# A two-layer Mamba/attention/mixture-of-experts kernel on one core: a scan group's output product summed in PSUM and copied by ScalarE, attention masks on GpSimd, packed attention averages

## The chip, the core and the metric

The kernel runs on one core of one Trainium2 chip. The metric is the device time of one execution in microseconds; three runs of the kernel before are known. The core has five queues of instructions: TensorE (PE, matmuls and their weight loads), VectorE (DVE), ScalarE (ACT), GpSimd (POOL) and SyncE (SP, which starts DMAs). Each runs its own instructions in the order in which they were written; between queues there are semaphores only. GpSimd works on SBUF tiles alone in this kernel.

## The reference, cut to what matters

Input x is 8 sequences of 256 tokens of 128 channels. Layer 0 normalises, runs a forward and a backward Mamba block and a top-2 mixture of experts and adds all up. Layer 1 runs a switch router with capacity 32 and its experts, and two attention blocks in a row. The parts that the change touches:

```python
# layer 0, for the forward and the backward direction
h = jnp.exp(dt_t[..., None] * A) * h + (dt_t * u_t)[..., None] * B_t[:, None, :]   # 16 states, 256 channels
y_t = jnp.einsum('bdn,bn->bd', h, C_t)
y = (y + u * Dp) * silu(z)
return jnp.einsum('bld,ed->ble', y, Wout)        # the output product; both directions are added to the rest
# layer 1, twice: global (causal) and then local (causal, window 32)
scores = jnp.einsum('bhqd,bhkd->bhqk', q, k) / np.sqrt(HD)     # 16 heads of 8, 4 key/value heads
scores = jnp.where(mask, scores, jnp.float32(-1e+30))
probs = softmax(scores);  out = jnp.einsum('bhqk,bhkd->bhqd', probs, v) @ wo
mask = (diff >= 0) & (diff < WIN)                # local; global is diff >= 0
```

## The kernel before, in words

**Scan stage.** Tokens are in four pairs of sequences (512 columns). A *scan group* g is one pair and one direction: groups 0 to 3 forward, 4 to 7 backward. Each group has 16 states N, and each state two halves of 128 channels. Per state and half, ACT computes the decays (line 878, in `decay`), POOL multiplies `dtu` by a broadcast row of B (line 682), DVE runs the scan (line 1203), and the result is multiplied by the row of C, half 0 by DVE (line 1211), half 1 by POOL (line 690). Of three states in four PE makes the drive of half 0 instead of POOL, as a matmul or a transpose (`turn_drive`, lines 1796 and 1798). PE sums the products over states in PSUM banks 4 and 5 (`add_y`, line 1818; line 1812 begins a group with the D term).

The rest of a group's work is spread over the states of the group before or after: depthwise convolution and projection u (lines 1728, 1776, 1779), z (1744), x (1748), dt (1752), all through one PSUM bank, `side`, that its users take in a fixed order (`SIDE`). Three states into a group DVE gates the previous group's sum (`gate_y`, line 1243), PE transposes it (line 1835), ACT copies it to `yT`, and PE's `finish` (line 1844) multiplies it by `Wout` into `side`, two matmuls for each of four token tiles. DVE then adds `side` to the running total `acc` (line 1255). ACT's Silu of u and z (lines 830, 832), between two table loads, stands in the same stretch, and so does dt: PE line 1752, ACT lines 851, 853, 855, DVE line 1185, after which POOL makes the next group's `dtu` (line 759).

`timeline()` writes out the order of this work once for PE and once for the readers of PSUM. `tensor_order` sets, for each state N, whether PE adds state N-3 or makes the drive of N+1 first: the drive is first where N modulo 16 is in `TURN_FIRST`.

**Attention stage.** 16 rounds b (8 global, then 8 local), one per sequence, each of three 128x128 blocks of keys and queries (`BLOCKS`: two on the diagonal, one under it, in that order), each block in two *units* of two key/value heads: 96 units. A unit is: PE writes a mask of 0 and -30000 into PSUM (lines 2077 and 2082; not for the full block under the diagonal) and adds the scores on top (lines 2088 and 2091), ACT takes the exponential into `probs` (line 1110, 1,024 elements per partition; 256 elements of 32 partitions for a local block under the diagonal, the *corner*). PE then averages the values, four matmuls of 512 columns per block (`average`, lines 2111 and 2114), into one bank for each 128 queries. Each such bank is copied by ACT (line 1117), transposed back by PE in four parts (line 2121) and divided by its row sums by DVE (lines 1634 and 1637). A matmul writes 32 rows per key/value head of which 9 hold values and the row sum. PE's, ACT's and DVE's preparation for later sequences (rms, T, L, Q, K, sqr, inv, split, turn) and the output projection (O1, O2) stand at places that `attention_timeline` gives. GpSimd only raises to the power -0.5 there (line 695).

## Time and profile before

| | us |
|---|---|
| median of 3 runs | 784.01 (783.31 to 787.82) |
| the profiled execution | 782.85, of which its span is 781.1 |
| the last scan of layer 0 ends | at 512.3 |
| router and experts of layer 1 | to 583.7 |
| attention: first to last exponential | 583.70 to 770.9 |
| after the last exponential | to 781.1 |

Over the span PE is busy 84%, DVE 75%, ACT 69% and POOL 53%; GpSimd does nearly nothing after 515 us. Times in rows are microseconds from the start of the span. In the rows below "x8" is eight merged instructions; a 128x128 float32 matmul that isn't a transpose shows as two of them. Durations of neighbours overlap a little, so what one instruction takes of its queue is read from two starts. The number in square brackets at a row's end is the time for which the engine had been idle, with what released it.

### The profile page before, as it was taken

To read this page: it belongs to the slowest core of one execution; us is meant where nothing else is said; L and a number is where in the kernel's file an instruction comes from. 1 tells how busy PE (TensorE), PEld (TensorE's weight loads), DVE (VectorE), ACT (ScalarE), POOL (GpSimd) and SP (SyncE) were. 2 spreads that over 40 slices of the span, in tenths; PEclk is the share of its full clock that TensorE was granted. 3 is DMA by queue.
4 is the path that set the end of the run, shared out by engine and by line. 5 is a ranking of instruction groups with operands and counts; after the bars stand their busy time and mean duration, and the time that the engine had idled before them with its cause. 6 is when DMAs were issued, how large, how long until landed. Compare 5 with 4: busy or idle time off the path is not lost.

```text
span 781.1 us, 13600 instructions
## 1 busy us (share of the span) xinstructions
PE 657.2 (84%) x4531; PEld 478.5 (61%) x4531; DVE 585.5 (75%) x863; ACT 540.6 (69%) x1021; POOL 416.9 (53%) x362
## 2 busy tenths in 40 slices
PE   4899977889898797888888967789888788888986
PEld 2588946658676585676776757677673334344433
DVE  7435679998999999999999998983335545655542
ACT  3465475877969878688798897825637757766663
POOL 6400168898998999989999899930000000000000
PEclk8799999899999999999999998999999999989998
DMA  6323577577596886857868668720200000000000
GB/s 199 109 82 115 153 165 214 164 206 222 151 248 184 195 255 152 231 181 178 258 168 221 205 156 235 198 108 28 82 1 0 2 1 2 1 1 2 15 14 28
DMA packets 81412, 100.15 MB, mean 128 GB/s; under 512 B 32560, under 2 KB 37816, under 8 KB 81344
## 3 DMA queue, kind: packets, MB, share of 16 engines
q1 hardware_dynamic: 81344, 99.29, 45.2%
q8 instruction: 37, 0.61, 0.3%
q14 instruction: 31, 0.25, 0.1%
HBM read 96.12 MB, written 3.24 MB: 127 GB/s over the span
## 4 chain that ended last, share of the span: by engine, by line
PE 43%; DVE 18%; issue 18%; ACT 13%; POOL 7%; DMA 0%; DVEq 0%; POOLq 0%; ACTq 0%
DVE ps L1203 5%; PE ps L1818 5%; PE ps L1869 3%; DVE hc L1211 3%; DVE moe L1203 3%; POOL drive L682 3%; PE ps L1884 3%; POOL hc L690 3%; PE ps L1796 3%; PE ps L2114 3%; PE ps L1748 2%; PE ps L1844 2%; PE ps L2091 2%; PE ps L1728 2%; PE ps L2021 2%
## 5 line engine op out<-in xcount | busy, mean ns | idle before, releaser
L682 POOL TENSOR_TENSOR drive<-dtu,b_sb 128x512 f32<-128x512 f32 x160 | 203.1, 1278 | 0.5 <-PE ps L1818 0.4
L690 POOL TENSOR_TENSOR hc<-moe,c_sb 128x512 f32<-128x512 f32 x128 | 163.3, 1276 | 19.2 <-DVE moe L1203 18.9
L1203 DVE TENSOR_TENSOR_SCAN moe<-ps,drive 128x512 f32<-128x512 f32 x128 | 153.4, 1199 | 0.0
L1818 PE MATMUL ps<-ident,hc 128*128 128x128 f32 x1024 | 139.3, 284 | 0.6 <-POOL hc L690 0.6
L1818 PEld LDWEIGHTS ps<-ident,hc 128*128 128x128 f32 x1024 | 122.5, 147 | 25.8 <-issue 19.9
L1110 ACT ACTIVATE probs<-ps 128x1024 f32<-128x1024 f32 (+1 forms) x96 | 87.6, 915 | 62.6 <-PE ps L2091 50.8
L878 ACT ACTIVATE ps<-dt,negA 128x510 f32<-128x510 f32 x160 | 106.5, 677 | 29.2 <-DVE moe L1203 28.5
L1203 DVE TENSOR_TENSOR_SCAN ps<-decay_sb,ps 128x512 f32<-128x512 f32 x96 | 117.2, 1221 | 12.4 <-PE ps L1796 11.6
L695 POOL TENSOR_TENSOR stat<-stat,halfc 128x4 f32<-128x4 f32 x7 | 7.1, 1008 | 190.9 <-DVE stat L1472 190.9
L1211 DVE TENSOR_TENSOR hc<-ps,c_sb 128x512 f32<-128x512 f32 x128 | 85.3, 666 | 0.0
L878 ACT ACTIVATE decay_sb<-dt,negA 128x510 f32<-128x510 f32 x96 | 68.3, 711 | 16.3 <-DVE ps L1203 16.3
L1796 PE MATMUL ps<-xm,dtuT 128*128 128x128 f32 x384 | 56.2, 293 | 12.2 <-DVE hc L1211 12.0
L909 ACT ACTIVATE scaled<-dtuT,bT 128x128 f32<-128x128 f32 x192 | 60.1, 389 | 0.6 <-PE ps L1798 0.6
L1796 PEld LDWEIGHTS ps<-xm,dtuT 128*128 128x128 f32 x384 | 51.0, 207 | 14.7 <-issue 14.7
L2114 PE MATMUL ps<-probs,v_ring 128*32 128x512 f32 x320 | 44.4, 626 | 8.6 <-DVE moe L1637 8.6
L1798 PE MATMUL ps<-ident,scaled 128*128 128x128 f32 x192 | 30.1, 280 | 25.5 <-DVE hc L1211 25.0
L1605 DVE CAST qT<-ps 128x512 f16<-128x512 f32 x32 | 22.1, 689 | 29.8 <-PE ps L2012 29.7
L1798 PEld LDWEIGHTS ps<-ident,scaled 128*128 128x128 f32 x192 | 22.1, 145 | 32.4 <-issue 24.9
L1203 DVE TENSOR_TENSOR_SCAN ps<-ps,drive 128x512 f32<-128x512 f32 x32 | 39.1, 1222 | 2.0 <-ACT ps L878 2.0
L813 ACT ACTIVATE hT<-ps,wbuf 128x256 f32<-128x256 f32 x64 | 25.8, 476 | 16.2 <-PE ps L1869 16.2
L768 POOL TENSOR_TENSOR seqstat<-seqstat,halfc 128x2 f32<-128x2 f32 x8 | 5.6, 698 | 58.3 <-DVE seqstat L1401 58.3
L1884 PEld LDWEIGHTS ps<-wbuf,hT 128*128 128x128 f32 x256 | 30.8, 192 | 3.1 <-issue 2.5
(281 smaller groups left out, 1224.3 us busy)
## 6 DMA issues: line engine op xcount, KB each, us to landing
b_sb<-bc_rows SPq DMA_DIRECT2D x128, 256.0 KB, 4.0
c_sb<-bc_rows SPq DMA_DIRECT2D x128, 256.0 KB, 4.0
xm<-spot_rows SPq DMA_DIRECT2D x48, 256.0 KB, 4.3
wbuf<-in_pack SPq DMA_DIRECT2D x16, 514.0 KB, 3.4
wbuf<-in_pack SPq DMA_DIRECT2D x8, 512.0 KB, 5.0
spot_rows<-c_sb SPq DMA_DIRECT2D x6, 256.0 KB, 4.5
x_sb<-in_x SPq DMA_DIRECT2D x4, 256.0 KB, 3.7
out<-x_sb SPq DMA_DIRECT2D x4, 256.0 KB, 2.3
```

The lines of the kernel that those rows point to most:

```text
L682: pool.tensor_tensor(drive_of(N, half), dtu[:, N // STATES % 2, half], b_sb[:, N % B_RING], ALU.mult) \
L690: pool.tensor_tensor(hc[:, 2 * (N % DEEP) + half], h_of(q), c_sb[:, N % C_RING], ALU.mult).then_inc(sem["hc_pooled"], 1)
L878: act.activation(seqs(decay_bank(q))[:, :, lo:lo + SEQ - 1], seqs(dt[:, g % 2, half])[:, :, lo:lo + SEQ - 1], ACT.Exp, scale=negA[:, g // ...
L909: last = act.activation(scaled[:, n % 2, block], dtuT[:, block], ACT.Copy, scale=bT[:, t, j:j + 1])
L1110: act.activation(probs[keys, t % 3, heads_u, 0:width], ps[keys, heads_u, 0:width], ACT.Exp, scale=HD ** -0.5).then_inc(sem["probs_ready"], 1)
L1203: dve.tensor_tensor_scan(h_of(q)[:, turn], decay_bank(q)[:, turn], source[:, turn], 0.0, ALU.mult, ALU.add).then_inc(sem["scan_done"], 1)
L1211: dve.tensor_tensor(hc[:, 2 * (N % DEEP)], h_of(q), c_sb[:, N % C_RING], ALU.mult).then_inc(sem["hc_ready"], 1)
L1796: last = pe.matmul(ps[:, H_BANKS[N % OWN_H], block], dtuT[:, block], spots[:, n % SPOT_RING, block], start=True, stop=True)
L1798: last = pe.transpose(ps[:, H_BANKS[N % OWN_H], block], scaled[:, n % 2, block], ident[:])
L1818: last = pe.matmul(ps[:, Y_BANK + half, block], hc[:, 2 * (N % DEEP) + half, block], ident[:], start=False, stop=True, is_transpose=True, ...
L1884: last = pe.matmul(bank[:, t * D:(t + 1) * D], hT[:, k, c, t * P:(t + 1) * P], wbuf[:, r, HIDDEN + CHUNKS + c * D:HIDDEN + CHUNKS + (c + 1 ...
L2114: last = pe.matmul(ps[g, AV_BANK + qt], v, probs[:, t % 3, kv], start=(t % 3 < 2), stop=(t % 3 != 1))
```

## The change

- `finish` on PE, for groups 0 to 6, adds `acc` into the same PSUM bank with four more matmuls by the identity, and ACT copies the bank to `acc` or `x_sb`. For groups 0 to 5 the copy stands in `side_part` between the Silu of u and that of z; for 6 it has a place of its own. DVE keeps the addition of group 7 alone.
- `TURN_FIRST` gains states 5 and 9, and DVE's `gate_y` stands before the scan of half 0, no longer between the halves.
- No mask goes through PE. After the exponential GpSimd sets what is hidden to zero in `probs`, in place, with `affine_select` (the function `hide`): one pass for each diagonal unit of the global rounds, two with a wait between them for the local ones, one small pass for a local corner unit. `average` waits for it, and stands one unit later in PE's order. Three loads of masks go.
- Averages are packed: heads go in two groups of 256 columns, the second with its values 16 rows higher (`VPAD`), so that one bank holds both 128-query halves of a sequence. There are eight matmuls of 256 columns per block for four of 512, and one ACT copy, one set of four transposes and one reciprocal per round for two.
- In attention `rms`, `T`, the copies and the order of k and q in `split` move; T, L and O1 are read before the exponential of their slot.

```diff
-TURN_FIRST = (4, 6, 8)
+TURN_FIRST = (4, 5, 6, 8, 9)
...
-        for n, at in ((2 * b, 4), (2 * b + 1, 8)):
-            put(6 * b + at + 2, "back", n)
-            put(6 * b + at, "copy", n)
+        put(6 * b + 11, "back", b)
+        put(6 * b + 9, "copy", b)
...
-        if at % 2 and 1 < at <= UNITS1 + 1:
-            unit.append(("average", at // 2 - 1))
-        first = [ev for ev in here if ev[0] == "turn"]
+        if at % 2 == 0 and 2 < at <= UNITS1 + 2:
+            unit.append(("average", at // 2 - 2))
+        first = [ev for ev in here if ev[0] in ("turn", "T", "L", "O1")]
...
+            def hide(U):
+                t = U // 2
+                l, own = t >= 3 * SEQS, BLOCKS[t % 3] != (0, 1)
+                if not l and not own:
+                    return
+                pool.wait_ge(sem["probs_ready"], U + 1)
+                after(pool, "probs_seen", seen_before(U))
+                heads_u = slice(2 * (U % 2), 2 * (U % 2) + 2)
+                keys, n = (slice(0, P), P) if own else (slice(P - WINDOW, P), WINDOW)
+                p = probs[keys, t % 3, heads_u, 0:GROUP * n].rearrange("p g (j q) -> p g j q", j=GROUP)
+                rows = [[0, 2], [0, GROUP]]
+                if own:
+                    first = pool.affine_select(p, p, rows + [[1, n]], ALU.is_ge, 0.0, base=0, channel_multiplier=-1)
+                    if not l:
+                        first.then_inc(sem["probs_seen"], 1)
+                        return
+                    first.then_inc(sem["probs_cut"], 1)
+                    pool.wait_ge(sem["probs_cut"], cut_before(U) + 1)
+                pool.affine_select(p, p, rows + [[-1, n]], ALU.is_ge, 0.0, base=WINDOW - 1 if own else -1, channel_multiplier=1) \
+                    .then_inc(sem["probs_seen"], 1)
...
                     act.activation(u_s[:, g % 2], u_s[:, g % 2], ACT.Silu).then_inc(sem["u_ready"], 1)
+                    if g > 1:
+                        finish(g - 2)
                     act.wait_ge(sem["side_free"], SIDE["z", g, 1] + 1)
...
+            def finish(g):
+                act.wait_ge(sem["side_ready"], SIDE["finish", g] + 1)
+                act.activation((x_sb if g >= PAIRS else acc)[:, 4 * (g % PAIRS):4 * (g % PAIRS) + 4],
+                               side.rearrange("p (t d) -> p t d", d=D), ACT.Copy).then_inc(sem["side_free"], 1)
...
+                if N > STATES and N % STATES == LAG:
+                    gate_y(N // STATES - 1)
                 scan(N, 0)
                 turn_boundary(2 * N)
-                if N > STATES and N % STATES == LAG:
-                    gate_y(N // STATES - 1)
                 scan(N, 1)
...
                     for half in range(HALVES):
                         last = pe.matmul(side[:, t * D:(t + 1) * D], yT[:, half, t * P:(t + 1) * P],
-                                         w_out[:, g // PAIRS, half], start=(half == 0), stop=(half == HALVES - 1))
+                                         w_out[:, g // PAIRS, half], start=(half == 0), stop=(half == HALVES - 1 and g == STEPS - 1))
+                    if g < STEPS - 1:
+                        if g < PAIRS:
+                            pe.wait_ge(sem["ln0_added"], SEQS)
+                        else:
+                            pe.wait_ge(sem["side_free"], SIDE["finish", g - PAIRS] + 1)
+                        last = pe.matmul(side[:, t * D:(t + 1) * D], ident[:], acc[:, 4 * (g % PAIRS) + t], start=False, stop=True)
...
-                        for rows in HALF_ROWS:
-                            keys = rows if kv == kvs[0] else HALF_ROWS[rows is HALF_ROWS[0]]
-                            pe.matmul(ps[keys, kv], ident16[rows, rows],
-                                      masks[rows, l if kv == kvs[0] else 3 + l].unsqueeze(1).broadcast_to([P // 2, GROUP, P]),
-                                      start=True, stop=False)
...
                 pe.wait_ge(sem["probs_ready"], 2 * t + 2)
+                pe.wait_ge(sem["probs_seen"], seen_before(2 * t + 2))
...
-                if t % 3 < 2:
-                    after(pe, "heads_done", 2 * (b - 1) + qt + 1)
+                if t % 3 == 0:
+                    after(pe, "heads_done", 2 * (b - 1))
```

The first place is PE in scan group 3, from the second transpose of the gated sum (line 1835) to the projection x. Before (L1844 is `finish`, L1748 x, L1752 dt, L1796 a drive):

```order
L1835 MATMUL ps<-ident,yg 128x128 x4
L1818 MATMUL ps<-ident,hc 128x128 x8
L1744 MATMUL ps<-w_in,xmT 128x128 x4
L1818 MATMUL ps<-ident,hc 128x128 x8
L1796 MATMUL ps<-xm,dtuT 128x128 x4
L1744 MATMUL ps<-w_in,xmT 128x128 x4
L1796 MATMUL ps<-xm,dtuT 128x128 x4
L1818 MATMUL ps<-ident,hc 128x128 x8
L1844 MATMUL ps<-w_out,moe 128x128 x8
L1818 MATMUL ps<-ident,hc 128x128 x8
L1796 MATMUL ps<-xm,dtuT 128x128 x4
L1748 MATMUL ps<-u_s,w_x 104x512 x2
```

The same stretch of PE in the changed kernel, where line 1884 is `finish`, 1891 its new matmuls, 1836 a drive and 1858 a sum:

```order
L1784 MATMUL ps<-w_in,xmT 128x128 x4
L1836 MATMUL ps<-xm,dtuT 128x128 x4
L1858 MATMUL ps<-ident,hc 128x128 x8
L1784 MATMUL ps<-w_in,xmT 128x128 x4
L1836 MATMUL ps<-xm,dtuT 128x128 x4
L1858 MATMUL ps<-ident,hc 128x128 x8
L1884 MATMUL ps<-w_out,moe 128x128 x2
L1891 MATMUL ps<-acc,ident 128x128
```

The drive of state 6 now stands before a sum, not behind it, and `finish` is four times (two matmuls and one more). Between `finish` and dt the order holds the same work as before, with the drive of state 10 one sum earlier.

The second place is PE in the attention stage, about one global round. Before, a diagonal unit is line 2082 (masks) and 2091, and each round has two sets of line 2121:

```order
L2114 MATMUL ps<-probs,v_ring 32x512 x4
L2121 MATMUL ps<-ident,avT 128x128 x4
L2012 MATMUL ps<-ident,qs 128x128 x4
L2091 MATMUL ps<-qT,kT 128x512 x4
L2114 MATMUL ps<-probs,v_ring 32x512 x4
L2121 MATMUL ps<-ident,avT 128x128 x4
L2012 MATMUL ps<-ident,qs 128x128 x4
L2082 MATMUL ps<-masks,ident 64x512 x4
L2091 MATMUL ps<-qT,kT 128x512 x2
```

In the changed kernel (2127 scores, 2155 averages, 2163 transposes back, 2058 and 2052 turns):

```order
L2155 MATMUL ps<-probs,v_all 32x256 x8
L2052 MATMUL ps<-ident,ks 128x128 x2
L1998 MATMUL ps<-w_kvu,latT 128x64 x4
L2127 MATMUL ps<-qT,kT 128x512 x2
L2058 MATMUL ps<-ident,qs 128x128 x4
L2127 MATMUL ps<-qT,kT 128x512 x2
L2155 MATMUL ps<-probs,v_all 32x256 x8
L2163 MATMUL ps<-ident,avT 128x128 x4
L2127 MATMUL ps<-qT,kT 128x512 x2
```

There are no rows for masks, eight short matmuls stand for four long ones, and one set of transposes back belongs to a round.

The third place is GpSimd in the local rounds, where before it had nothing but line 695. One round is now (line 798 the first pass, 804 the second and that of the corner):

```order
L798 AFFINE_SELECT probs<-probs 128x1024
L804 AFFINE_SELECT probs<-probs 128x1024
L798 AFFINE_SELECT probs<-probs 128x1024
L804 AFFINE_SELECT probs<-probs 128x1024
L798 AFFINE_SELECT probs<-probs 128x1024
L804 AFFINE_SELECT probs<-probs 128x1024
L798 AFFINE_SELECT probs<-probs 128x1024
L804 AFFINE_SELECT probs<-probs 128x1024
L804 AFFINE_SELECT probs<-probs 32x2x128 x2
```

Eight passes over 1,024 elements and two over 256 are what a local round adds to that queue.

## Rows read from the trace of the kernel before

**Rows 1.** Windows: us; busy PE, PEld, DVE, ACT, POOL; clock, DMA. Scan, global, local.
```profile
275.50:324.50 49.00, 41.49 (x274) 32.23 (x272) 47.76 (x57) 39.06 (x75) 46.88 (x39) 0.97 0.76 203
583.70:679.87 96.17, 79.08 (x646) 35.31 (x646) 53.39 (x111) 68.31 (x94) 4.03 (x4) 0.98 0.00 1
679.87:770.90 91.03, 80.62 (x699) 40.06 (x699) 46.70 (x101) 60.86 (x91) 2.02 (x2) 0.94 0.04 10
```

**Rows 2.** Timeline, DVE in scan group 3: start, duration, instruction, idle time before it.
```profile
272.72 1.27 DVE L1243 TENSOR_TENSOR yg<-ps,z_s 128x512 f32<-128x512 f32 x2
...
282.07 1.23 DVE L1203 TENSOR_TENSOR_SCAN ps<-decay_sb,ps 128x512 f32<-128x512 f32 x1 [0.72 <-PE ps L1796]
...
287.78 0.69 DVE L1255 TENSOR_TENSOR acc<-acc,ps 128x512 f32<-128x512 f32 x1
288.39 1.23 DVE L1203 TENSOR_TENSOR_SCAN ps<-ps,drive 128x512 f32<-128x512 f32 x1
```

**Rows 3.** The chain of waits through the same group, start, us, what.
```profile
283.21 1.21 DVE moe L1203
...
285.70 2.05 PE ps L1844 x16
287.75 0.87 PE ps L1818 x8
288.62 0.89 PE ps L1796 x8
289.51 1.72 PE ps L1748 x4
...
296.80 0.72 ACT decay_sb L878
...
297.54 0.07 DVE ps L1203
```

**Rows 4.** Timeline, DVE's longest waits for PE in groups 1, 4 and 7.
```profile
179.69 1.23 DVE L1203 TENSOR_TENSOR_SCAN ps<-decay_sb,ps 128x512 f32<-128x512 f32 x1 [1.09 <-PE ps L1796]
183.80 1.23 DVE L1203 TENSOR_TENSOR_SCAN ps<-decay_sb,ps 128x512 f32<-128x512 f32 x1 [1.19 <-PE ps L1796]
333.02 1.23 DVE L1203 TENSOR_TENSOR_SCAN ps<-decay_sb,ps 128x512 f32<-128x512 f32 x1 [1.02 <-PE ps L1796]
480.88 1.23 DVE L1203 TENSOR_TENSOR_SCAN ps<-decay_sb,ps 128x512 f32<-128x512 f32 x1 [1.41 <-PE ps L1796]
```

**Rows 5.** Timeline, PE at the gate of groups 3 and 4.
```profile
273.54 0.63 PE L1835 MATMUL ps<-ident,yg 128*128 128x128 f32 x4 [1.82 <-DVE yg L1243]
...
324.61 0.66 PE L1835 MATMUL ps<-ident,yg 128*128 128x128 f32 x4 [0.78 <-ACT u_s L822]
```

**Rows 6.** Lines by form, global rounds, then local: count, busy, mean ns, idle before.
```profile
L2114 PE MATMUL ps<-probs,v_ring 128*32 128x512 f32 x176 | 24.3, 624 | 4.4 <-DVE moe L1637 4.4
...
L2114 PE MATMUL ps<-probs,v_ring 128*32 128x512 f32 x144 | 20.1, 629 | 4.2 <-DVE moe L1637 4.2
...
L2077 PE MATMUL ps<-masks,ident 128*32 128x128 f16 x32 | 4.6, 224 | 0.0
```

**Rows 7.** Timeline, PE in the global rounds.
```profile
641.04 0.41 PE L2082 MATMUL ps<-masks,ident 64*64 64x512 f16 x4
641.38 0.39 PE L2091 MATMUL ps<-qT,kT 32*128 32x512 f16 x2
...
642.70 0.66 PE L2121 MATMUL ps<-ident,avT 128*128 128x128 f32 x4
643.19 0.39 PE L2012 MATMUL ps<-ident,qs 128*128 128x128 f16 x4
```

**Rows 8.** Timeline, GpSimd: one fill of 512 and of 1,024 elements.
```profile
0.74 0.53 POOL L642 MEMSET c_sb<- 128x512 f32 x1 [0.29 <-POOLq L2214]
...
525.75 0.95 POOL L775 MEMSET v_ring<- 128x1024 f32 x1
```

**Rows 9.** The page's costliest groups: GpSimd's product of two tiles.
```profile
L690 POOL TENSOR_TENSOR hc<-moe,c_sb 128x512 f32<-128x512 f32 x128 | 163.3, 1276 | 19.2 <-DVE moe L1203 18.9
```

More of the change, by code:

```diff
@@ L267, in attention_timeline @@
         unit = [("unit", at)] if 0 <= at < UNITS1 else []
-        if at % 2 and 1 < at <= UNITS1 + 1:
-            unit.append(("average", at // 2 - 1))
-        first = [ev for ev in here if ev[0] == "turn"]
+        if at % 2 == 0 and 2 < at <= UNITS1 + 2:
+            unit.append(("average", at // 2 - 2))
+        first = [ev for ev in here if ev[0] in ("turn", "T", "L", "O1")]
         order += here + unit
-        readers += first + unit + [ev for ev in here if ev[0] != "turn"]
+        readers += first + unit + [ev for ev in here if ev not in first]
     return order, readers
@@ L291, with seen_before, cut_before @@
 PREP = {ev: n for n, ev in enumerate(ev for ev in FILL + AT_ORDER if ev[0] in ("T", "L", "Q", "K", "O1", "O2"))}
+def seen_before(U):
+    return sum(V // 2 >= 3 * SEQS or V // 2 % 3 < 2 for V in range(U))
+def cut_before(U):
+    return sum(V // 2 >= 3 * SEQS and V // 2 % 3 < 2 for V in range(U))
 def shared_before(q):
@@ L780, in _ @@
                     rms_pow(ev[1])
+                    pool.wait_ge(sem["rms_pow"], ev[1])
+                elif ev[0] == "unit":
+                    hide(ev[1])
         @block.scalar
@@ L983, in _ @@
                     copy_y(ev)
+                elif ev == ("finish", STEPS - 2):
+                    finish(STEPS - 2)
                 elif ev[0] == "xt":
@@ L2001, in turn @@
                 first = 2 * (b % 2)
-                pe.wait_ge(sem["qk_split"], 2 * G + 2)
+                pe.wait_ge(sem["qk_split"], 2 * G + (2 if part else 1))
                 after(pe, "turn_copied", TURN["turn", b, part])
@@ L2115, in average, with turn_back @@
                 last.then_inc(sem["av_done"], 1)
[L2117 to L2121 removed]
+            def turn_back(b):
+                pe.wait_ge(sem["av_copied"], b + 1)
+                for n in range(4):
+                    last = pe.transpose(ps[:, AV_BANK + b % 2, n * P:(n + 1) * P], avT[:, b % 2, n * P:(n + 1) * P], ident[:])
```

116 lines of the change are left out of this document (54 added, 62 removed).

## The prediction

> **What bounds the kernel now.** I read the windows by stage first. In a scan group of 49.0 us DVE is busy 47.8 and POOL 46.9 [rows 1]: DVE sets the pace there, and every microsecond in which it waits is lost. In the attention rounds no engine is full, but PE comes nearest: 79.1 of 96.2 us in the global rounds and 80.6 of 91.0 in the local ones, with ACT at 68.3 and 60.9 and POOL at 4.0 and 2.0 [rows 1]. There TensorE and ScalarE hand units to each other, and GpSimd is free.
>
> The timeline of DVE in the scan shows one recurring gap, the wait for the drive of state 6, 0.72 us in group 3 [rows 2], and more in groups 1, 4 and 7: 1.09 and 1.19, 1.02, 1.41 [rows 4]. Group 6 repeats group 1 within 0.01, groups 2 and 5 repeat group 3, group 7 has 0.16 more. That makes 9.3 us in all.
>
> The chain of waits shows what else is tight. From the scan at 283.21 it runs over ACT's decay and copy of z, then on PE without a hole over `finish` (285.70), a sum, a drive, x (289.51), two sums, a drive and dt, ends on ACT with the decay at 296.80 (0.72 us), and lets DVE's scan go at 297.54, 0.02 us behind it [rows 3]. DVE itself had no gap between its own scans there. So two strings of equal length run side by side in that stretch of every group but the last: DVE's own work, with the addition of `finish` in it, and the PE-ACT string, with the matmuls of `finish` in it.
>
> **The scan stage, part by part.**
>
> *The addition leaves DVE.* It takes 0.61 us of its queue, from 287.78 to 288.39 [rows 2]. But it stood on one of two equal strings, and the other grows: `finish` gets four more float32 matmuls of 128x128. Four such matmuls are one drive, 0.89 us [rows 3]. PE goes from `finish` to dt without idling, so dt comes 0.9 later and DVE waits, first at a decay that ACT now makes late, then at dt. ACT's copy of the bank, 0.5 us and a wait of about 0.8 for PE before it, falls in the time for which the x projection is awaited anyway, so it adds nothing to the string. Groups 1 to 6: +0.9 x 6 = +5.4 us. Group 7 has no dt, there DVE gains its 0.6. If the string had slack that I don't see, the six groups would give 0.6 each back instead: bounds -3.6 and +5.4, and I take +5.4, as the slack shown is 0.02. Net +4.8.
>
> *The gate moves ahead of the scan of half 0.* The two gate operations begin at 272.72 and the scan before them is one pitch earlier, 1.1 us. PE had been idle for 1.82 us when they came [rows 5], so all that follows on PE, up to the drive of state 6, comes 1.1 earlier. In group 4 the transposes were released by ACT's copy of u, not by the gate [rows 5], so nothing moves there.
>
> *The drive of state 6 goes before a sum.* A sum of eight transposes is 0.87 [rows 3], which is what the drive gains. Together 2.0 us, or 0.9 in group 4. Groups 2, 3, 5 and 7 then lose their whole gap (0.7 x 3 + 1.6), groups 1 and 6 2.0 of 2.3 each, group 4 0.9 of 1.0: -8.6 us. POOL has 2.1 us to spare in a group and doesn't stop this. Bounds: 0 (another wait lies right behind) to -9.3. I take -8.6, since the idle before the gate is longer than the shift.
>
> Scan stage: +4.8 - 8.6 = **-3.8 us**.
>
> **The attention stage.**
>
> *Masks off PE.* Four mask matmuls take 0.34 us of the queue, from 641.04 to 641.38 [rows 7]. 32 diagonal units in each half of the stage: -10.9 in the global rounds, as much in the local ones. The 16 corner units had 32 small ones, busy 4.6 us with overlaps [rows 6]; I take 3.5.
>
> *Packing.* A set of transposes back takes 0.49 (642.70 to 643.19) [rows 7], eight fewer in each half, -3.9. The waits of the average for DVE's division of the bank, 4.4 in the global rounds and 4.2 in the local ones [rows 6], go, since the next round has a bank of its own. Against it stand four more matmuls in each of 48 averages with the same columns. I put 0.1 each, between 0 and the 0.5 of a whole set of four transposes: +2.4 a half. ACT also gets rid of 16 copies, DVE of 16 small operations; they bound nothing.
>
> *Global rounds.* 10.9 + 3.9 + 4.4 - 2.4 = 16.8 us come off PE. ACT with 68.3 busy in 96.2 becomes the neighbour, so not all is won: the same sum times PE's busy share, 0.82, is 13.8, and the earlier T and L would add a little. **-15**, bounds -10 and -22.
>
> *GpSimd's passes.* No row shows `affine_select`. The nearest below is a fill, one stream, 0.95 us for 1,024 elements [rows 8]; from 512 to 1,024 it grows by 0.42, so 0.11 is fixed. The nearest above is a product of two tiles, 1.28 for 512 [rows 9], thus 2.5 for 1,024. A pass has one tile to read and one to write, and a comparison of the position; it is nearer to the fill, and I take c = 1.1. For what lies between two passes, each with a wait, I add 0.1, as much as the fixed part of a fill. In the global rounds 32 passes are 38 us of 81 and hide behind units.
>
> *Local rounds.* PE without masks needs 91.0 - 10.9 - 3.5 - 3.9 - 4.2 + 2 = about 71 us. GpSimd needs 64 x 1.2 + 16 corner passes at a quarter of the elements, 16 x 0.46, + 2 for its powers [rows 1] = 86.2. **GpSimd is the new bound**, and the local rounds take 86.2, not 91.0: **-4.8**; bounds -14 (c = 0.95) and +90 (c = 2.5). What waits behind a late pass is the average on PE's queue, and with it the scores behind it.
>
> *Tail.* After the last unit there is a pass, a longer average and both halves of the output in one copy: **+1**, bounds 0 and 3.
>
> *Loads.* Three loads of masks fewer at the end of the scan, hidden beside it: 0. The router and experts get the L projection of the second preparation instead of the attention stage: 0.
>
> **Sum.** 782.85 - 3.8 - 15 - 4.8 + 1 = 760.3 for an execution like the profiled one, which is 1.2 below the median shown: **761.5 us**.
>
> **The rivals.**
>
> *GpSimd is slow and the kernel is slower.* Each microsecond more on c makes the local rounds longer by 64 + 4 = 68 us. The total is back at 784 when c is 1.43. With c in the middle of the two rows, 1.73, it is 761 + 43 = 804; with 2.5 it would be 857. For it: two passes per local unit on one queue, and the only arithmetic on full tiles that GpSimd shows runs at more than twice the time per element of the fill. Against: those have two inputs, this has one. By over 1% it is slower from c = 1.55 on; chance **0.20**.
>
> By the Trainium skill (GPSIMD Engine Reference, 3.1) the tight loop of a one-input operation is bound by its ports at 1.03 cycles of 1.2 GHz per element for up to two operations, and takes at best about 1.8 for three or more. No row here shows which holds for a mask that depends on position. By the first c would be an estimated 0.99 and the sum about 754, by the second an estimated 1.65 and the sum about 799.
>
> *About the same.* c between 1.31 and 1.55, or c of 1.1 with half of the rest lost, because DVE stands at `rms` until GpSimd's power comes, which now queues behind passes, and the turned copies that PE needs stand behind it. 776 to 792. Six such waits of some 2 us are possible; DVE is idle 43 us of the global rounds [rows 1], which speaks against it. Chance **0.13**.
>
> *The scan gives nothing.* The gaps of groups 1, 6 and 7, longer than the others [rows 4], show PE slower behind the gate there; if it gets slower still, only half of the 8.6 comes back: +4.8 - 4.3, total 766. This lies inside the forecast's range.
>
> *More than forecast.* c at the fill's 0.95 makes GpSimd's local sum 76, the dt string turns out to have slack, and the global rounds give 20: 761 - 10 - 8 - 5 = 738. Chance of less than 740: **0.05**.
>
> *The move does not do what it says.* The addition is meant to leave the bound engine, but its matmuls land on an equal string. That is in the forecast already.
>
> **How the numbers follow.** Forecast case, 740 to 776, 0.62; more than forecast 0.05; about the same 0.13; slower 0.20. The likeliest case gives 761.5. The range leaves out 0.05 below 740 and some 0.13 above 800: 740 to 800. A change of 1%, 8 us, is what these runs can tell. Faster by over 1% (below 776) 0.67, within 1% 0.13, slower 0.20.
>
> **What the changed profile would show.** A pass of 1,024 elements near 1.1 us, GpSimd busy over 9 tenths of the local rounds and PE idle there at the averages, released by GpSimd; DVE in the scan without gaps before state 6, but with new waits of half a microsecond or more for ACT's decays and at dt, some 0.9 us later after the copy of z than before; groups 2, 3 and 5 as long as before within 0.3 us, groups 1 and 6 shorter by over 1. The prediction is wrong if a pass is far from 1.1 us, if PE's saving in the global rounds comes back as ACT's, or if dt doesn't move.

## The result, and the profile after

The change made the kernel slower by 0.6%: 788.39 us (785.0 to 790.44, 20 runs) against 783.17 for the kernel before, a ratio of 1.0063 with a 95% interval of 1.0045 to 1.008. The forecast was 761.5. The profiled execution took 786.54 us, its span is 784.7 (781.1 before).

To compare stages over all kernels, I cut the span at two events that every one of them has: the first exp of attention and the first corner exp (32x256, four units into the local rounds); the last cut is the end of the last exp. These are the windows of the kernel before (from the first exp to the first corner exp, which I call the global stretch; to the end of the last exp, the local stretch; to the end, the tail; columns as in [rows 1]):

```profile
583.70:690.37 106.67, 89.09 (x734) 40.36 (x734) 58.29 (x122) 75.89 (x103) 4.03 (x4) 0.98 0.00 1
690.37:770.90 80.53, 70.62 (x613) 35.01 (x611) 41.80 (x90) 53.27 (x82) 2.02 (x2) 0.94 0.04 11
770.90:781.10 10.20, 3.83 (x30) 2.65 (x28) 2.48 (x6) 1.19 (x2) 0.00 (x0) 0.74 0.09 26
```

And of the changed kernel:

```profile
577.33:674.20 96.87, 78.25 (x750) 40.89 (x754) 59.87 (x114) 70.55 (x94) 47.01 (x41) 0.91 0.00 1
674.20:770.05 95.85, 66.54 (x618) 36.98 (x607) 46.26 (x83) 49.29 (x74) 79.18 (x76) 0.74 0.03 9
770.05:784.70 14.65, 6.79 (x48) 4.30 (x48) 2.50 (x7) 1.19 (x2) 1.94 (x3) 0.50 0.06 18
```

All up to the first exp is 6.4 us shorter, the global stretch 9.8 shorter, the local one 15.3 longer and the tail 4.5 longer: +3.6. In the local stretch GpSimd (fifth busy column) goes from 2 to 79 us, TensorE does 4 us less, and its granted clock falls from 0.94 to 0.74.

**The scan** went as the working had it. DVE's waits from 150 to 500 us in the kernel before, by what it waited for (total us, times, longest); the first line sums [rows 4] and their like:

```profile
DVE ps L1203 <- PE ps L1796: 9.3, 10, 1.4
DVE ps L1203 <- ACT decay_sb L878: 0.7, 2, 0.6
```

and after, where the drive of state 6 has lost its wait and the new ones are at ScalarE's decays and at dt:

```profile
DVE ps L1245 <- ACT decay_sb L918: 3.8, 8, 0.5
DVE moe L1245 <- ACT ps L918: 2.9, 6, 0.5
DVE dt L1227 <- ACT dt_a L889: 2.0, 6, 0.3
DVE ps L1245 <- ACT ps L918: 1.5, 1, 1.5
DVE ps L1245 <- PE ps L1836: 0.3, 1, 0.3
```

This window leaves out group 0. There the kernel before has 2.3 us more than every other profile of this document, and it isn't the code: run 10, which has the scan as before, takes 52.34 us for the group where the kernel before takes 54.70, and TensorE's clock differs. The same ten microseconds in the kernel before, then in run 10:

```profile
120.00:130.00 10.00, 7.87 (x52) 7.24 (x51) 9.90 (x14) 4.34 (x7) 7.91 (x8) 0.83 0.63 193
```

```profile
120.00:130.00 10.00, 7.87 (x64) 6.89 (x63) 9.90 (x14) 4.25 (x7) 7.90 (x8) 1.00 0.71 207
```

So of the 6.4 us ahead of the first exp 2.3 seem to belong to the profiled execution of the kernel before and not to the change.

**A pass** takes 1.09 us alone and 1.17 on average, where the forecast took 1.1. GpSimd's groups in the attention stage (count, busy, mean ns, idle before):

```profile
L798 POOL TENSOR_SCALAR_AFFINE_SELECT probs<-probs 128x1024 f32<-128x1024 f32 x64 | 74.6, 1165 | 82.2 <-ACT probs L1152 56.9 <-issue 20.1
L804 POOL TENSOR_SCALAR_AFFINE_SELECT probs<-probs 128x1024 f32<-128x1024 f32 x32 | 37.6, 1175 | 2.2
L804 POOL TENSOR_SCALAR_AFFINE_SELECT probs<-probs 32x256 f32<-32x256 f32 x16 | 10.0, 625 | 6.2 <-ACT probs L1152 4.2 <-POOL probs L804 0.4
```

**What holds the local rounds** shows at the `rms` of the last but one preparation. GpSimd, then DVE, then TensorE in the same 15 us (start, duration, instruction, idle before it):

```profile
688.45 1.09 POOL L798 TENSOR_SCALAR_AFFINE_SELECT probs<-probs 128x1024 f32<-128x1024 f32 x1
689.62 1.09 POOL L804 TENSOR_SCALAR_AFFINE_SELECT probs<-probs 128x1024 f32<-128x1024 f32 x1
690.68 1.01 POOL L702 TENSOR_TENSOR stat<-stat,halfc 128x4 f32<-128x4 f32 x1
691.76 0.96 POOL L804 TENSOR_SCALAR_AFFINE_SELECT probs<-probs 32x256 f32<-32x256 f32 x1
694.83 0.45 POOL L804 TENSOR_SCALAR_AFFINE_SELECT probs<-probs 32x256 f32<-32x256 f32 x1 [2.12 <-ACT probs L1152]
```

```profile
688.50 1.07 DVE L1511 TENSOR_SCALAR stat<-stat 128x4 f32<-128x4 f32 x1
691.72 0.69 DVE L1517 TENSOR_TENSOR xm<-acc,stat 128x512 f32<-128x512 f32 x1 [2.15 <-POOL stat L702]
```

```profile
687.46 0.66 PE L2163 MATMUL ps<-ident,avT 128*128 128x128 f32 x4
692.55 1.09 PE L1994 MATMUL ps<-ident,xm 128*128 128x128 f32 x4 [4.44 <-DVE xm L1517]
...
694.87 1.94 PE L2155 MATMUL ps<-probs,v_all 128*32 128x256 f32 x16
696.73 2.08 PE L2000 MATMUL ps<-w_q,xmT 128*128 128x128 f32 x8
```

DVE's variance (line 1511) is ready at 689.57, but GpSimd still has passes and reaches the power (line 702) at 690.68; `xm` follows at 691.72, T on TensorE at 692.55. T stands ahead of scores in TensorE's queue, so no unit is made meanwhile, and then GpSimd, the engine that was late, has nothing to do: 2.12 us at 694.83, and again at 696.07 and 700.48. TensorE comes out of the hole at its lower level: T takes 1.09 where it takes 0.63 elsewhere in the same kernel, an average 1.94 where it takes 1.07.

Two more readings bear on this. DVE waits for the power 1.12 us in each of the four preparations of the global rounds, and 2.15 and 5.75 us in the two of the local ones. And of the 10.2 us for which GpSimd waits in the local stretch 9.6 lie in the 9 us behind these two `xm`; from 730 us on, when nothing is prepared any more, it waits 0.6 us in all. What TensorE waits for most in the local stretch are the passes, at the averages, as the prediction said:

```profile
PE ps L2155 <- POOL probs L804: 14.7, 7, 3.2
PE ps L1994 <- DVE xm L1517: 8.0, 2, 4.4
```

### The profile page after: what moved, and what is told of

Read it like the earlier page. It is cut to its first block and busy times, and to the rows that moved or that the text cites. A ratio compares the mean times of both kernels' runs of the same rounds, so it can differ in the third digit from the quotient of the medians.

```text
span 784.7 us, 13926 instructions
## 1 busy us (share of the span) xinstructions
PE 646.9 (82%) x4619; PEld 482.7 (62%) x4619; DVE 586.2 (75%) x840; ACT 534.4 (68%) x1012; POOL 537.3 (68%) x474
## 5 line engine op out<-in xcount | busy, mean ns | idle before, releaser
L798 POOL TENSOR_SCALAR_AFFINE_SELECT probs<-probs 128x1024 f32<-128x1024 f32 x64 | 74.6, 1165 | 82.2 <-ACT probs L1152 56.9
L918 ACT ACTIVATE ps<-dt,negA 128x510 f32<-128x510 f32 x160 | 106.4, 677 | 26.3 <-DVE moe L1245 25.5
L1152 ACT ACTIVATE probs<-ps 128x1024 f32<-128x1024 f32 (+1 forms) x96 | 85.3, 915 | 43.5 <-PE ps L2127 32.7
L1253 DVE TENSOR_TENSOR hc<-ps,c_sb 128x512 f32<-128x512 f32 x128 | 84.9, 663 | 0.0
L918 ACT ACTIVATE decay_sb<-dt,negA 128x510 f32<-128x510 f32 x96 | 68.3, 711 | 15.3 <-DVE ps L1245 15.3
L2155 PE MATMUL ps<-probs,v_all 128*32 128x256 f32 x640 | 52.5, 454 | 21.2 <-POOL probs L804 16.4
L1836 PE MATMUL ps<-xm,dtuT 128*128 128x128 f32 x384 | 52.9, 282 | 11.1 <-DVE hc L1253 11.1
L1836 PEld LDWEIGHTS ps<-xm,dtuT 128*128 128x128 f32 x384 | 47.4, 194 | 14.6 <-issue 14.6
L804 POOL TENSOR_SCALAR_AFFINE_SELECT probs<-probs 128x1024 f32<-128x1024 f32 (+1 forms) x48 | 47.6, 992 | 8.4 <-ACT probs L1152 4.2
L2155 PEld LDWEIGHTS ps<-probs,v_all 128*32 128x32 f32 x640 | 19.7, 122 | 40.2 <-issue 26.1
```

The source lines that it names most:

```text
L798: first = pool.affine_select(p, p, rows + [[1, n]], ALU.is_ge, 0.0, base=0, channel_multiplier=-1)
L804: pool.affine_select(p, p, rows + [[-1, n]], ALU.is_ge, 0.0, base=WINDOW - 1 if own else -1, channel_multiplier=1) \
L918: act.activation(seqs(decay_bank(q))[:, :, lo:lo + SEQ - 1], seqs(dt[:, g % 2, half])[:, :, lo:lo + SEQ - 1], ACT.Exp, scale=negA[:, g // ...
L1152: act.activation(probs[keys, t % 3, heads_u, 0:width], ps[keys, heads_u, 0:width], ACT.Exp, scale=HD ** -0.5).then_inc(sem["probs_ready"], 1)
L1253: dve.tensor_tensor(hc[:, 2 * (N % DEEP)], h_of(q), c_sb[:, N % C_RING], ALU.mult).then_inc(sem["hc_ready"], 1)
L1836: last = pe.matmul(ps[:, H_BANKS[N % OWN_H], block], dtuT[:, block], spots[:, n % SPOT_RING, block], start=True, stop=True)
```

## Experiments

Each run stands beside runs of the kernel before on the same chip, and the ratio is to those. Runs 1, 3 and 5 form a ladder from the kernel before to the changed one. A step between two runs of the ladder is good to some 3 or 4 us by their intervals. Windows are of one profile each: the global stretch of the changed kernel is 96.87 us, and those of runs 9, 5 and 7, which differ from it only in how the last four units of the stretch are masked, are 99.76, 99.98 and 102.28. So differences of up to 5 us between single global stretches prove nothing.

**1. The scan part alone** (the attention stage of before):

```
-TURN_FIRST = (4, 6, 8)
+TURN_FIRST = (4, 5, 6, 8, 9)
...
+   last = pe.matmul(side[:, t * D:(t + 1) * D], ident[:], acc[:, 4 * (g % PAIRS) + t], start=False, stop=True)
```

> The kernel before with the scan part of the change alone (the sum of finish on TensorE with ScalarE's copy, the gate ahead of the scan of half 0, the drive of state 6 ahead of the sum); its attention stage is that of before. In the changed kernel's profile the first exp of attention begins 6.4 us earlier. If the scan part is what it looks like there, this is 777 us, 5 to 7 below the kernel before. Rival: the attention stage of the kernel before starts from another phase and takes some back, or the scan's gain there came with the other edits (the fill of the router and experts): 780 or more.

780.43 us, ratio 0.9953 (0.9928 to 0.9977), so -3.7 us; the forecast's term was -3.8. I had expected 777. The profiled run has the first exp at 577.96, 5.7 us earlier than before (2.3 of it in group 0), the same global stretch (106.70), and a local stretch and a tail that are 1.3 and 0.8 longer (81.85 and 10.99).

**2. The two moves of order alone**, `finish` added by DVE as before:

```
-TURN_FIRST = (4, 6, 8)
+TURN_FIRST = (4, 5, 6, 8, 9)
...
+if N > STATES and N % STATES == LAG:
+    gate_y(N // STATES - 1)
 scan(N, 0)
 turn_boundary(2 * N)
-if N > STATES and N % STATES == LAG:
-    gate_y(N // STATES - 1)
 scan(N, 1)
```

> The kernel before with the two moves of order alone (the gate ahead of the scan of half 0, the drive of state 6 ahead of the sum), while DVE keeps the addition of finish. If the sum of finish on TensorE lengthens a string as long as DVE's own, as the prediction had it (+4.8), this is some 5 us below the run with the whole scan part: 771 to 773. Rival: DVE is the bound alone and the finish move is worth 0.6 a group: then it is 3 to 4 us above the run with the whole scan part, 780 to 781.

772.46 us, ratio 0.986 (0.9821 to 0.9898): -11.0. DVE's waits in the scan:

```profile
DVE ps L1203 <- PE ps L1796: 1.4, 2, 1.1
DVE ps L1203 <- ACT decay_sb L878: 0.7, 2, 0.5
```

2.1 us instead of 10.5 in the changed kernel. So the addition that leaves DVE costs 7.3 us (0.9953 - 0.986), because its matmuls lie on the string to dt. The theory that DVE alone is the bound falls. The length of each scan group, from its first scan to the next group's (us, one profile each):

| group | 0 | 1 | 2 | 3 | 4 | 5 | 6 | 7 |
|---|---|---|---|---|---|---|---|---|
| kernel before | 54.70 | 50.79 | 49.13 | 50.43 | 49.66 | 49.14 | 51.07 | 48.89 |
| run 10, scan as before | 52.34 | 50.79 | 49.13 | 50.41 | 49.66 | 49.13 | 51.06 | 48.81 |
| run 2 | 52.41 | 48.32 | 48.32 | 49.60 | 48.79 | 48.32 | 48.60 | 48.29 |
| run 1 | 52.36 | 49.21 | 49.21 | 50.48 | 49.31 | 49.21 | 49.51 | 48.98 |
| changed kernel | 52.41 | 49.21 | 49.22 | 50.48 | 49.78 | 49.22 | 49.50 | 48.31 |

In group 7 of run 1 DVE waits once for a late decay, which it doesn't in run 2:

```profile
DVE ps L1213 <- ACT ps L886: 1.6, 1, 1.6
```

**3. The masks back on TensorE**, all else of the change kept:

```
-   elif ev[0] == "unit":
-       hide(ev[1])
+   pe.matmul(ps[keys, kv], ident16[rows, rows], masks[rows, ...], start=True, stop=False)
```

> The changed kernel with the masks back on TensorE as in the kernel before, and all else of the change kept (scan part, packed averages, moved order of the attention stage). Theory 1 (GpSimd's passes lose the time): 783 - 6 for the scan - some 6 to 12 for the packing: 765 to 771, and the granted clock of the local rounds is back at 0.9. Theory 2 (moved order and packing lose it): 778 or more, with TensorE's waits of 2.6 us at T before DVE's xm still there in the global rounds.

772.31 us, ratio 0.9858 (0.9826 to 0.989), a little above the range of theory 1. Theory 2 falls: packing and the moved slots don't lose the time. Its windows, cut as above (this profiled execution, 768.83 us, was the shortest of its six):

```profile
577.14:684.12 106.98, 92.72 (x896) 45.01 (x896) 57.34 (x114) 71.17 (x93) 4.03 (x4) 0.92 0.01 1
684.12:756.95 72.83, 66.94 (x764) 35.45 (x764) 40.03 (x84) 49.11 (x74) 2.02 (x2) 0.95 0.04 12
```

Against the kernel before the local stretch is 7.7 shorter and the global one not at all.

**4. No passes at all**, no wait for them: the masking is left out.

```
-   hide(ev[1])
...
-   pe.wait_ge(sem["probs_seen"], seen_before(2 * t + 2))
```

> The changed kernel without any of GpSimd's mask passes and without the wait for them: it leaves the masking out. Theory 1 (the passes on GpSimd hold up the units, by their own sum in the local rounds and by standing ahead of GpSimd's power for rms): local rounds fall from 104.7 to about 72, global ones from 88.7 to about 82, the tail by 2: 745 to 752. Theory 2 (the moved order and the packed averages lose the time: rms and T two slots later, one copy for both halves): the global rounds stay at 88 and the local ones at 85 or more: 768 or above.

759.33 us, ratio 0.9673 (0.9636 to 0.9709). The passes of the change cost 0.039, 30 us. The local stretch is 71.97, the tail 10.12. Theory 1 had the total too low by 7, theory 2 too high by 9. The global stretch is 101.62 and so no shorter than with passes: TensorE still waits 2.7 to 2.8 us at T four times there. (This profiled execution, 763.75 us, was the longest of its six.)

**5. Passes in the global rounds, TensorE's masks in the local ones:**

```
-   if not l and not own:
+   if l or not own:
        return
```

> The changed kernel with GpSimd's passes in the global rounds alone and the masks on TensorE in the local ones. Theory 1 (the loss of the change sits in the local rounds, where GpSimd has two passes a unit): the stretch from the first corner exp to the last exp falls from 95.9 to the 72.8 of the run with all masks on TensorE, the tail from 14.7 to 10.1: 788.4 - 23 - 4.6 = 761; the global rounds keep the 96.9 from the first exp to the first corner exp. Rival (the clock: less work on TensorE leaves it at its low level, and what the masks cost comes back): 768 to 772, as with all masks on TensorE.

763.02 us, ratio 0.9727 (0.9693 to 0.976). In the global rounds the passes give 0.0131, 10 us, against TensorE's masks (run 3 less this run); in the local rounds they cost 0.0336, 26 us (1.0063 - 0.9727). The whole loss is there:

```profile
577.96:677.94 99.98, 82.08 (x772) 42.01 (x772) 60.28 (x114) 70.30 (x94) 42.13 (x36) 0.90 0.00 1
677.94:751.88 73.94, 67.93 (x764) 35.96 (x764) 40.03 (x84) 49.07 (x74) 2.01 (x2) 0.93 0.04 12
```

**6. rms and T earlier**, in the changed kernel:

```
-for name, at in (("rms", -15), ("T", -13), ...
+for name, at in (("rms", -17), ("T", -14), ...
```

> The changed kernel with the slots of rms and T back at -17 and -14, where the kernel before has them; all else of the change kept. TensorE waited at T for DVE's xm 2.6 to 2.8 us four times in the global rounds and 3.5 to 4.4 in the local ones. Theory 1 (the shorter way from rms to T makes the holes, and in the local rounds the passes that stand ahead of GpSimd's power make them longer): the global rounds fall by 5 to 11, the local ones by some 8: 770 to 776. Rival (in the local rounds GpSimd's passes are the bound by their sum alone): only the global part comes back, and the local rounds stay at 100 or more: 778 to 783.

785.81 us, ratio 1.0033 (1.0013 to 1.0053). Only 0.003, some 2 us, comes back: both readings had more, 770 to 776 and 778 to 783. The local stretch is 92.58 us. **The same with TensorE's masks:**

> The kernel with the masks back on TensorE and all else of the change, and with rms and T at -17 and -14. In the run without this edit TensorE waited 11.0 us at T for DVE's xm in the global rounds and 2.7 in the local ones. Theory 1: the holes go, and the granted clock in the rounds that had them rises: 8 to 12 us below that run's 772.3, 760 to 764. Rival (the holes took the place of waits of the same size elsewhere, 15 us of them in the kernel before for the division, the latent copy and the keys): within 2 us of 772.

769.93 us, ratio 0.9818 (0.9786 to 0.985), an interval that overlaps that of run 3. I had expected 760 to 764, or 770 to 774 if the slots do nothing. The slots are not the cause of the loss.

**7. One pass instead of two** on each whole local unit; the window's mask on the diagonal units is left out.

```
-   if not l:
-       first.then_inc(sem["probs_seen"], 1)
-       return
-   first.then_inc(sem["probs_cut"], 1)
-   pool.wait_ge(sem["probs_cut"], cut_before(U) + 1)
+   first.then_inc(sem["probs_seen"], 1)
+   return
```

> The changed kernel with one of GpSimd's two passes on each whole local unit; it leaves out the window's mask on the diagonal units. GpSimd's own sum in the local rounds falls from 84 to 84 - 32 x 1.2 = 46 us. Theory A (the sum of the passes is the bound there, with the holes at rms as their consequence, since a unit waits two passes): local from the first corner exp 73 to 76, total 762 to 766. Theory B (a pass of any number behind the exp makes the way from a unit to its average, and so rms to T, longer): local 82 or more, total 772 or above.

762.98 us, ratio 0.9764 (0.9744 to 0.9783); the local stretch is 68.47. Theory B falls: a pass behind the exp isn't the trouble, the second one is. The tail is 12.03.

**8. The power of rms on ScalarE** for groups 4 to 7, both passes kept:

```
+   elif kind == "pow":
+       act.wait_ge(sem["rms_var"], G)
+       act.activation(stat[:, 0, rows], stat[:, 2, rows], ACT.Ln).then_inc(sem["rms_ln"], 1)
+       act.wait_ge(sem["rms_ln"], G - 3)
+       act.activation(stat[:, 3, rows], stat[:, 0, rows], ACT.Exp, scale=-0.5).then_inc(sem["rms_pow"], 1)
```

> The changed kernel with the power of rms of groups 4 to 7 on ScalarE (Ln and Exp, as it does for q and k) in a slot of its own, so that it no longer stands behind GpSimd's passes. If the in-order queue of GpSimd makes the holes (TensorE waits at T 4.4 and 3.5 us for xm, ScalarE 8.7 at its longest for T, GpSimd idle for 10 us in the local rounds in all), GpSimd then runs through: local falls by 8 to 10, total 778 to 780. Rival (the holes come from the units' rate, as ScalarE's square and DVE's sums also queue behind late units): within 3 us of 788.

774.48 us, ratio 0.9923 (0.9896 to 0.995): 0.014, 11 us, where 8 to 10 were expected, by taking four instructions of 1.0 us off a queue and `xm` off the slot of the sums. GpSimd has the same passes. The two stretches:

```profile
578.07:670.81 92.74, 75.86 (x742) 39.02 (x746) 59.80 (x113) 71.22 (x98) 44.59 (x39) 0.93 0.01 1
670.81:758.35 87.54, 64.09 (x622) 36.30 (x621) 46.88 (x85) 50.42 (x78) 77.44 (x74) 0.80 0.04 10
```

From the end of ScalarE's square to its copy of T are 3.4 us here (684.92 to 688.30), 6.0 in the change (687.68 to 693.68):

```profile
684.29 0.63 ACT L1068 ACTIVATE sq<-acc 128x512 f32<-128x512 f32 x1
685.95 0.21 ACT L1071 ACTIVATE stat<-stat 128x4 f32<-128x4 f32 x1 [1.03 <-DVE stat L1518]
...
688.30 0.69 ACT L1076 ACTIVATE xmT<-ps,cols 128x512 f32<-128x512 f32 x1 [1.50 <-PE ps L2004]
```

The local stretch falls by 8.3; the 4.1 of the global one are within its scatter. What remains above the 72.8 with TensorE's masks is GpSimd's own sum: 77.4 busy, 3.1 in waits for exps, and the other 7 in gaps of some 0.1 between instructions. The waits were 10.2 in the change.

**9. Masks in both places** in the local rounds, to see what the low clock does:

```
+elif kt == qt and l:
+    for rows in HALF_ROWS:
...
+        pe.matmul(ps[keys, kv], ident16[rows, rows], masks[rows, ...], start=True, stop=False)
```

> The changed kernel with the masks of the local rounds on TensorE too, beside GpSimd's passes, so that TensorE has some 14 us of matmuls more there and GpSimd the same passes. The granted clock of the local rounds was 0.74 in the change and 0.95 with TensorE's masks. Theory C (the low clock of a TensorE that idles is what lengthens the local rounds): the added matmuls raise the clock and cost nothing or give time back, 780 to 788. Rival (the clock is only a consequence of GpSimd's bound; TensorE's work then adds in the holes, where it is on the path): 790 to 796.

789.68 us, ratio 1.0099 (1.0068 to 1.013), against 1.0063. TensorE is busy 77.3 of 95.1 us instead of 66.5 of 95.9, the clock goes from 0.74 to 0.82, and the stretch keeps its length. The total is 0.0036 higher, 3 us, and the two intervals overlap. So 11 us more of work on TensorE together with a clock raised by 0.08 changed nothing that can be told; that each of the two alone would do nothing is not shown. It fits a stretch that is GpSimd's.

**10. Packing alone**, everything else, slots too, as before (keys split ahead of queries, as the change has it).

> The kernel before with the packed averages alone (one bank and one copy a round, v with its pad, ks split first), the averages, rms, T and the readers' order in the slots of the kernel before. The run with TensorE's masks and all the other edits is 8.1 us below the run with the scan part alone. Theory P (packing gives what there is, in the local rounds): 783 - 8 = 775, from the first exp to the first corner exp 107 as before. Rival (packing gives 6 in the global rounds too, as forecast, and the later slots lose them): 768 to 771, the first stretch 101 to 103.

774.67 us, ratio 0.9899 (0.9869 to 0.9929), -7.9:

```profile
580.66:688.36 107.70, 92.99 (x897) 45.75 (x898) 56.89 (x113) 72.15 (x95) 4.03 (x4) 0.92 0.01 1
688.36:762.25 73.89, 68.04 (x760) 36.17 (x764) 41.02 (x84) 49.06 (x74) 2.01 (x2) 0.93 0.04 12
```

In the attention stage all of it is local, 6.6 us (3.0 more lie ahead of the first exp, 2.4 of them in group 0, and the tail is 0.8 longer). In the global stretch TensorE is busy 3.9 us more than before although eight sets of transposes have gone, its clock at 0.92 instead of 0.98. Its timeline there:

```profile
635.66 1.16 PE L1990 MATMUL ps<-w_q,xmT 128*128 128x128 f32 x8 [1.58 <-ACT latT L1064]
...
637.71 1.94 PE L2154 MATMUL ps<-probs,v_all 128*32 128x256 f32 x16
...
642.46 1.07 PE L2154 MATMUL ps<-probs,v_all 128*32 128x256 f32 x16
```

The eight matmuls right behind the wait still take 1.16 us; the average after them takes 1.94, and 5 us later the same takes 1.07.

**11. Global passes made twice**, TensorE's masks in the local rounds (as run 5 but for that):

```
+first.then_inc(sem["probs_cut"], 1)
+pool.wait_ge(sem["probs_cut"], seen_before(U) + 1)
+first = pool.affine_select(p, p, rows + [[1, n]], ALU.is_ge, 0.0, base=0, channel_multiplier=-1)
```

> The kernel with GpSimd's passes in the global rounds and TensorE's masks in the local ones, each global pass made twice. GpSimd then is busy some 42 + 38 = 80 of the first 100 us. If passes are free as long as their sum stays below the units' time, this is 763 to 765, as with single passes. Rival (a unit's second pass and the power behind it lengthen the way to T, as in the local rounds of the change): 770 or more, GpSimd idle meanwhile.

790.19 us, ratio 1.009 (1.0055 to 1.0125): 0.036, 28 us, above run 5.

```profile
578.74:705.76 127.02, 91.53 (x772) 45.89 (x772) 65.29 (x114) 71.79 (x94) 80.13 (x68) 0.77 0.00 1
```

GpSimd's sum, 80 us, would have fitted into the 100 us of run 5, and yet the stretch grew by 27 for 38 us of passes. What TensorE waits for in the global stretch shows where. First run 5, in which it never waits for a pass, then this run:

```profile
PE ps L1998 <- DVE xm L1521: 10.9, 4, 2.8
```

```profile
PE ps L2001 <- DVE xm L1524: 18.9, 4, 4.9
PE ps L2172 <- POOL probs L805: 10.0, 4, 3.1
```

The holes at T that were there grow by 8.0 us, and 10.0 us of waits at averages are new. DVE's four waits for the power are 2.15 to 3.37 us instead of 1.12. On GpSimd, here and then in run 5:

```profile
600.89 1.09 POOL L805 TENSOR_SCALAR_AFFINE_SELECT probs<-probs 128x1024 f32<-128x1024 f32 x1
601.96 1.01 POOL L706 TENSOR_TENSOR stat<-stat,halfc 128x4 f32<-128x4 f32 x1
609.57 1.10 POOL L802 TENSOR_SCALAR_AFFINE_SELECT probs<-probs 128x1024 f32<-128x1024 f32 x1 [6.61 <-ACT probs L1159]
```

```profile
594.83 1.01 POOL L706 TENSOR_TENSOR stat<-stat,halfc 128x4 f32<-128x4 f32 x1
602.15 1.10 POOL L802 TENSOR_SCALAR_AFFINE_SELECT probs<-probs 128x1024 f32<-128x1024 f32 x1 [6.31 <-issue]
```

GpSimd is idle for 6 us behind the power in both: the two units under the diagonal have no pass. So its passes come in bursts of four units, each with a pitch of 2.4 us when made twice, and much of the time between the bursts stays unused. Passes are free at one a unit, not at two.

**12. What beats both kernels.** The rms-early kernel with TensorE's masks and DVE's `finish`, then run 5 with DVE's `finish`, then that with the power of groups 2 to 7 on ScalarE:

> The kernel with the masks on TensorE and rms and T at -17 and -14, and with the addition of finish back on DVE (scan part: the two moves of order alone). The two runs of the scan part differ by 7 to 8 us. If that adds to the attention edits, this is 7.5 below the run with the same attention stage, 753 to 757; rival (the attention stage takes some back): 760 or more. It should beat both kernels.

> GpSimd's passes in the global rounds alone, TensorE's masks in the local ones, packed averages, the change's order, and the addition of finish back on DVE. With the scan's 7.5 and the attention stage of the mixed run: 763.0 - 7.5 = 755.5. Rival (the saving of the scan is partly taken back by the attention stage's phase, as in the run with TensorE's masks and rms early, 6.1 of 7.5): 757 to 759. It should beat every kernel so far.

> The fastest kernel so far (passes in the global rounds alone, finish on DVE) with the power of rms of groups 2 to 7 on ScalarE. In the changed kernel that move gave 13.9 us, of which 4 in the global rounds. If the way from rms to T costs there as well, 2 to 5 us below 755.2: 750 to 753. Rival (GpSimd's queue was the reason, and it is short here): 754 to 757.

They took 763.86 us, ratio 0.975 (0.9718 to 0.9783), above the 753 to 757 expected, so that DVE's `finish` gave 5 us there and not 7.5; 755.18, ratio 0.967 (0.9649 to 0.969); and **747.30, ratio 0.9575 (0.9539 to 0.9612)**, 4.2% faster than the kernel before. The last has 93.15 us for the global stretch and 70.00 for the local one, the second 95.78 and 75.55. So the edit of run 8, made for two groups more, gives 0.0095, 7 us, also where GpSimd has one pass a unit or none: it seems that a good part of what it gives is the shorter way from rms to T, not the queue.

## Why the prediction was wrong

In us of the kernel before (ratios by 783), the ladder gives what each part is worth, beside the forecast's term:

| part | forecast | measured | runs |
|---|---|---|---|
| scan: gate and state 6 | -8.6 | -11.0 | 2 |
| scan: finish on TensorE | +4.8 | +7.3 | 1, 2 |
| packing (and slots) | about -11 | -7.4 | 1, 3 |
| masks of the global rounds | about -9 | -10.3 | 3, 5 |
| masks of the local rounds, tail | about +2 | +26.3 | 5, change |

The forecast's own terms go by stage, so the last three are split here from its working: 5.9 x 0.82 + 6 for packing, 10.9 x 0.82 for the global masks, and 86.2 against the 84.9 that TensorE would need locally with its masks (91.0 - 3.9 - 4.2 + 2), plus 1 for the tail. Each measured part is good to some 3 or 4 us.

**The scan was right**, in mechanism and sum: the waits moved as foretold, from state 6 to the decays and dt; in group 3 ScalarE reads dt 10.79 us after it began the copy of z, 9.90 before; groups 2, 3 and 5 are as long as before within 0.1 us, 1 and 6 shorter by 1.6. And -3.7 stands beside -3.8. By the ratios each of the two parts is 2.5 larger, which their intervals allow. By the lengths of the groups 1 to 7 the moves of order give 8.9 us, where 8.6 was forecast, and `finish` costs 5.0 in groups 1 to 6, for a forecast of 5.4. Wrong was group 7: 0.6 should have come back there, but against run 2 nothing does in the change and 0.7 is lost in run 1, since a decay is late.

**The pass was right.** c is 1.17 for the 1.1 taken; a unit of two passes has a pitch of 2.4, as forecast. The corner pass is 0.63, not 0.36, +4 in all. The first rival, slow GpSimd, would have needed c of 1.43, and is out.

**The step that failed is "GpSimd is the new bound, and the local rounds take 86.2".** It took the sum of an engine's work for the time of a stage. From the 49th exp, the first of a local unit, the local rounds took 103.4 us. GpSimd was busy for 84.1 of them and in small gaps for 6.8, which is 4.7 more than forecast and nearly all corner passes; for the other 12.5 it waited. "Busy over 9 tenths" came out as 8. Its passes come in a queue together with the power of rms, which the preparation waits for, which TensorE waits for at T, ahead of the scores that feed GpSimd. An engine near its bound that also serves the loop that feeds it is late with the service and then starves. Run 11 makes the waits for the power and the holes at T longer in the global rounds as well.

The other half of the step is what 86.2 was compared with. The 91.0 of [rows 1] begins with the 47th exp; from the 49th the kernel before takes 87.9. And packing, by the forecast's own terms, takes 6.1 off that without any pass: 81.8, where run 3 measured 81.6. Beside this 86.2 is a loss of 4.4 us from the start. Of the stretch from the first corner exp the 23.0 us between the change and TensorE's masks (95.85 and 72.83) are 13 of GpSimd's sum (79.2 busy and 7 of gaps, against 72.8) and 10 of its waits; the tail has the other 4.6. Run 8 gives 8.3 of that stretch back, as the waits fall from 10.2 to 3.1; run 7 all of it, as the sum falls to 42.

**The right rival was named and priced too low.** "DVE stands at `rms` until GpSimd's power comes" had 0.13 and a span of 776 to 792, and held the result. Against it I put that DVE is idle for 43 us in the global rounds [rows 1]. But idle time of DVE is no slack on the way over it: what counts is what stands behind T in TensorE's queue. The rival had six such waits of some 2 us in mind; two, of 2.15 and 5.75, with the starving behind them, were enough.

**The global rounds.** "Hide behind units" holds for one pass a unit (run 5). But -15 came out as -9.8 in the changed kernel's profile and as -4.4 to -6.9 in runs 5, 7 and 9. The discount by PE's busy share was too kind to packing: it gives nothing there (run 10). Shown is that TensorE then waits for DVE and ScalarE between preparations and that its clock is 0.92 for 0.98; that these take what packing saves is argued. The four added matmuls of an average, put at 0.1 each, cost nothing: 16 of 256 columns take 1.07 us, eight of 512 took 1.06.

**The tail** was put at +1, bounds 0 and 3, and is 14.65 instead of 10.20. Its clock is 0.50, the lower level throughout, and it keeps 14.65 in run 8. That passes make it so shows in run 5 (10.32) and run 4 (10.12).

Not settled: how low clock and waits share what packing loses in the global rounds, since no run changed the clock alone there; and how much of run 8's 11 us is the queue, since the edit gave 7 without one and the intervals of the two overlap. At the place shown the queue itself holds the power for 1.1 us, from 689.57 to 690.68.

## What to carry to other kernels

Before work goes to an idle engine, list what that engine already does for the others, and follow each such small instruction to what stands behind it: a 1.0 us power of four columns, late by a pass or two, went to ScalarE for 11 us here, and for 7 where it was not late. Compare the sum of the new bound with what the stage would take without the move, not with what it takes now. Work that leaves the engine that paces a stage gains nothing if it lands on a string of the same length.

## What the runs showed of the hardware

The granted clock follows the holes, though not each and not at once. In the change four transposes took 1.09 us behind waits of 4.44 and 3.53 us, and 0.63, as elsewhere, behind the four waits of 2.6 to 2.8 in the global rounds. Eight float32 matmuls 4 us after the first of these took 2.08 instead of 1.16. The longer times are those of the lower of the clock's two levels, 1.2 GHz instead of 2.4. In run 10, behind a wait of 1.58, eight matmuls took 1.16 and the average after them 1.94 instead of 1.07. TensorE with less to do can be busy longer: 93.0 us with packed averages against 89.1. Yet in the local rounds of the change, where GpSimd sets the pace, a higher clock and 11 us of added matmuls together made no difference beyond 3 us.

GpSimd's power on 128x4 values takes 1.01 us, about as long as its pass over 128x1024 (1.09). ScalarE's Ln and Exp of the same values take 0.21 each.

A small instruction of DVE can last as long as a pass beside it. The variance on 128x4 values takes 0.17 or 0.18 us in the four global preparations of the change; at 688.50 it took 1.07 and ended at 689.57, when the pass that had begun at 688.45 ended too (689.54). At 715.03 it took 0.59 and ended at 715.62, again with a pass (715.60).
